# Second attention: the multiplication of the probabilities by their inverse sums moves from VectorE to GpSimd

## The reference, cut to what matters

```python
def _L1_xattn_ref(q, kv, x_seqlens, Wq, Wk, Wv, Wo, q_norm_w, k_norm_w):
    DIM, HEADS, HEAD_DIM = (128, 16, 64)
    qh = (q @ Wq).reshape(b, l, HEADS, HEAD_DIM).transpose(0, 2, 1, 3)
    kh = (kv @ Wk).reshape(b, s, HEADS, HEAD_DIM).transpose(0, 2, 1, 3)
    vh = (kv @ Wv).reshape(b, s, HEADS, HEAD_DIM).transpose(0, 2, 1, 3)
    qh = rms_norm(qh, q_norm_w)          # x * rsqrt(mean(x^2) + 1e-5) * w, over a head's 64
    kh = rms_norm(kh, k_norm_w)
    scores = jnp.einsum('bhld,bhsd->bhls', qh, kh) * (1.0 / np.sqrt(HEAD_DIM))
    scores = jnp.where(mask, scores, NEG_INF)
    attn = jax.nn.softmax(scores, axis=-1)
    o = jnp.einsum('bhls,bhsd->bhld', attn, vh)
    return o.transpose(0, 2, 1, 3).reshape(b, l, HEADS * HEAD_DIM) @ Wo
...
x = x + tanh(g_xattn[1]) * _L1_xattn_ref(_layernorm(x), ctx_1024, _lenS2, ...)
```

## Time and profile before

| what | value |
|---|---|
| median of 3 runs | 2186.36 us |
| the 3 runs | 2183.57 to 2186.93 us |
| the profiled execution: its own time | 2186.99 us |
| the profiled execution: its span | 2185.2 us |
| PE busy, share of the span | 1930.7 us, 88% |
| DVE busy | 1592.2 us, 73% |
| ACT busy | 811.0 us, 37% |
| POOL busy | 662.1 us, 30% |
| second attention, first probabilities turned to last | 842.1 to 1320.1 us |

### The profile page before, as it was taken

How to read it: one execution, slowest core, us unless ns; L and a number is a source line. 1 busy time by engine, 2 the same in 40 slices (tenths; PEclk the granted TensorE clock), 3 DMA queues, 4 the chain that set the end, 5 groups by cost and what they waited for, 6 DMA issues and landing times. The chain is left out here.

```text
span 2185.2 us, 41654 instructions
## 1 busy us (share of the span) xinstructions
PE 1930.7 (88%) x14275; PEld 1025.3 (47%) x14275; DVE 1592.2 (73%) x3255; ACT 811.0 (37%) x1491; POOL 662.1 (30%) x903
## 2 busy tenths in 40 slices
PE   4659998998998978999999998979997999979965
PEld 2644444444444434555555554435663444436631
DVE  4768868878878866777777775757884666658978
ACT  4632112012012105555565553315652222226645
POOL 4551102102102104555555553445730000022301
PEclk8559999999999989999999999989997999999966
DMA  4402222222222231000000000000002533311001
GB/s 112 147 18 60 54 45 59 52 45 59 52 45 59 54 83 65 2 2 1 0 0 0 0 2 1 1 6 16 15 6 63 138 79 105 85 38 19 15 1 39
DMA packets 60079, 89.66 MB, mean 41 GB/s; under 512 B 23720, under 2 KB 42024, under 8 KB 55472
## 3 DMA queue, kind: packets, MB, share of 16 engines
q1 hardware_dynamic: 59952, 88.04, 16.4%
HBM read 80.85 MB, written 2.97 MB: 38 GB/s over the span
## 5 line engine op out<-in xcount | busy, mean ns | idle before, releaser
L1021 PE MATMUL l0f_acc<-l0f_z,w_all 128*128 128x512 f32 x512 | 228.8, 609 | 15.0 <-DVE l0f_z L1229 15.0
L916 POOL TENSOR_TENSOR l0f_v<-l0f_val,l0f_top 64x256 f32<-64x256 f32 x128 | 78.2, 611 | 488.1 <-DVE l0f_val L1191 479.5
L970 PE MATMUL l0f_work<-w_all,l0f_xs 128*128 128x512 f32 x384 | 183.5, 600 | 15.2 <-DVE l0f_val L1186 14.5
L1021 PEld LDWEIGHTS l0f_acc<-l0f_z,w_all 128*128 128x128 f32 x512 | 99.1, 195 | 144.1 <-issue 124.2
L241 POOL TENSOR_SCALAR var_eps<-mean_var 128x4 f32<-128x4 f32 (+1 forms) x64 | 14.6, 227 | 474.3 <-DVE mean_var L225 472.2
L1415 PE MATMUL l1x_proj_v<-l1x_wvo,l1x_cs 128*64 128x512 f32 x512 | 134.9, 605 | 0.1
L1191 DVE COPY_PREDICATED l0f_val<-l0f_oh,l0f_work 128x512 f32<-128x512 int32 x160 | 116.6, 729 | 23.7 <-PE l0f_work L970 7.5
L2826 DVE TENSOR_TENSOR l2f_hu<-l2f_act_g,l2f_pu 128x512 f32<-128x512 f32 x104 | 71.1, 684 | 68.8 <-ACT l2f_act_g L2752 67.4
L2752 ACT ACTIVATE l2f_act_g<-l2f_pg 128x512 f32<-128x512 f32 x104 | 61.5, 594 | 149.8 <-PE l2f_pu L2693 138.0
L2701 PE MATMUL l2f_acc<-l2f_hid,w_all 128*128 128x512 f32 x208 | 107.6, 599 | 10.3 <-DVE l2f_hid L2832 10.3
L1641 DVE TENSOR_TENSOR l1x_nm_q<-l1x_proj_q,l1x_rs_q 128x512 f32<-128x512 f32 x64 | 44.2, 691 | 90.3 <-POOL l1x_rs_q L1351 90.3
(11 more groups left out here) (389 smaller groups left out, 4413.1 us busy)
## 6 DMA issues: line engine op xcount, KB each, us to landing
l0f_first_mask<-onehots SPq DMA_DIRECT2D x32, 512.0 KB, 5.7
w_all<-onehots SPq DMA_DIRECT2D x32, 512.0 KB, 11.8
w_all<-combination SPq DMA_DIRECT2D x40, 256.0 KB, 5.3
w_all<-in_weights SPq DMA_DIRECT2D x1, 4640.0 KB, 16.7
l0x_m_b<-running_max SPq DMA_DIRECT2D x16, 256.0 KB, 4.6
w_all<-combination SPq DMA_DIRECT2D x16, 224.0 KB, 4.5
w_all<-combination SPq DMA_DIRECT2D x16, 192.0 KB, 4.2
w_all<-combination SPq DMA_DIRECT2D x16, 160.0 KB, 4.3
```

The lines of the kernel that those rows point to most:

```text
L916: nc.gpsimd.tensor_tensor(v2[a * SEQ:(a + 1) * SEQ, t % 2, b, :, :], val[r, t % 2, :, :].rearrange("p (c a) k -> p c a k", a=2)[:, :, a, : ...
L970: nc.tensor.matmul(value_banks[e % 3][:, :], xs[:, t * P:(t + 1) * P], ve[:, e, :], start=True, stop=True).then_inc(ve_done, 1)
L1021: nc.tensor.matmul(acc[:, :], oe[:, n % E, n // E, :], z[:, n % Z, :], start=(n == 0), stop=(n == C * E - 1)).then_inc(acc_done, 1)
```

## The change

scale_probs leaves VectorE's program and becomes an instruction of GpSimd. On VectorE the slot loses one instruction, and on GpSimd the slot gains one, ahead of inverse_q, so behind the two inverse roots of the slot before. It waits there for inv_done, and signals prob_ready, as VectorE's did. Operands, shapes and types are the same.

```diff
@@ GpSimd @@
+                def scale_probs(n):
+                    pool.wait_ge(inv_done, count(n + 1))
+                    nc.gpsimd.tensor_tensor(prob[:, :, :], prob[:, :, :], bcast(inv[:, :], 2, SEQ), ALU.mult)\
+                        .then_inc(prob_ready, 1)
+
                 def slot(g, j):
+                    h, i = lagging(g, j, 2)
+                    if live(h):
+                        scale_probs(U * h + i)
                     if live(g):
                         inverse_q(U * g + j)
...
@@ VectorE @@
-                def scale_probs(n):
-                    dve.wait_ge(inv_done, count(n + 1))
-                    nc.vector.tensor_tensor(prob[:, :, :], prob[:, :, :], bcast(inv[:, :], 2, SEQ), ALU.mult)\
-                        .then_inc(prob_ready, 1)
-
...
                     h, i = lagging(g, j, 2)
                     if live(h):
                         totals(U * h + i)
-                        scale_probs(U * h + i)
```

## The result

| | median us | range | runs |
|---|---|---|---|
| before | 2186.24 | 2183.57 to 2189.07 | 10 |
| with the change | 2175.16 | 2167.11 to 2179.32 | 10 |

The account below looks back on a forecast made before the run. TensorE was taken to wait on a circle through VectorE and GpSimd in the second attention. Gains of 12.3 and 0.3 less 1.0 at the ends make 11.6 us: 2186.99 to 2175.4, median-adjusted to 2175; range 2169 to 2187.

Parts of the forecast that it names:

- The bound: Second attention: a circle through VectorE and GpSimd makes TensorE wait 0.59, 1.54, 0.13 us behind copy, residual, xn slots.
- The price: GpSimd's moved multiplication of 128x512 takes 1.04 us, where VectorE took 0.69.
- The rivals of 1.27 and 1.85: GpSimd's multiplication takes 1.27 us: no gain, 2187, chance 0.10; or is held up to 1.85: 2223, chance 0.10.
- The hand-over: From VectorE's reciprocal to GpSimd's multiplication 0.20 us, so start of inv to turn_probs grows from 0.99 to 1.50.
- the copy stretch: From the turn_probs of the copy slot to the next: 7.55 us becomes 7.47, gain 0.08.
- The residual slot: Stretch behind it: addition to x and ms_q move up beside GpSimd's multiplication; 8.50 us becomes 7.89, gain 0.61.
- The norm and the xn slot: Stretches behind them: norm stays at TensorE's 7.23 us, gain 0; xn falls from 7.09 to TensorE's 6.96, gain 0.13.
- The ends: In front of the first and the last turn_probs nothing hides the hand-over: 2 x 0.51 us lost.
- The sum: Second attention: 12.3 us from 15 units, 0.3 from the first unit, less 1.0 at both ends: gain 11.6.
- The other signs: In the profile after, VectorE's idle time before nm_q grows, and proj_q and scores find no new wait.
- The two engines in each other's way: xn slot: GpSimd's multiplication stretches the first xn to 0.75 us, at no cost; rival, pow holds the second: 2186, chance 0.04.
- The twofold price for two inputs: Skill's rule against the move: two-input elementwise work costs GpSimd twice VectorE's time; estimated 1.12 us, sum about 9.

Follow-up runs that it names:

- the run with both moves: Changed kernel with the addition to x behind the sum of squares of q and GpSimd's staging copies behind inverse_k: 2155.11 us, ratio 0.9859 to the kernel before.

## Why the prediction was right, and where its sum was off

*The bound.* Right. The chain through the moved multiplication and GpSimd's inverse root set three of four stretches; with it out of the way TensorE's own 6.96 and 7.18 are what is left (the run with both moves).

*The price.* 1.04, as taken from the broadcast multiplication of line 1814, 64 times within 4 ns. The rivals of 1.27 and 1.85 fall.

*The hand-over.* Mis-sized. 0.20 between VectorE's end and GpSimd's start was taken from ms_q; behind the reciprocal it is 0.08 (900.65 to 900.73, and in all 64 slots). So inv to turn_probs is 1.38, not 1.50, and the copy stretch, which hangs on it in full, is 7.32 instead of 7.47. That is 0.22 of gain instead of 0.08, some 2 us over 15 units.

*The residual slot.* Predicted 7.89, measured 7.73 where the slots are written out, 0.12 of it the hand-over. In the loop it is 7.98. There the addition starts 0.24 to 0.26 after inv, where it is 0.12 in the written-out slots; before, it started 0.61 after the multiplication in both:

```profile
1017.95 0.20 DVE L1678 RECIPROCAL l1x_inv<-l1x_tot 128x8 f32<-128x8 f32 x1
1018.20 0.48 DVE L1683 SCALAR_TENSOR_TENSOR x_all<-l1x_y,tanh_g,x_all 128x256 f32 x1
```

In the loop the tile of x is given by a register (core.x[:, bass.ds(2 * pair, 2), :]), so the likely cause is address work that the multiplication used to cover; register work isn't in the profile, and no run isolates it. The prediction read its rows in written-out slots alone and has no such term. Another 0.1 goes between the addition's start and the end of ms_q (2.03 written out, 2.16 in the loop), most of which was there before too (2.07, 2.15). Against 8.50 to 8.58 the gain is 0.6 to 0.8, near the forecast 0.61, as the two errors are of opposite sign.

*The norm and the xn slot.* 0.13 forecast for xn, 0.13 measured as a mean, though from 7.10 (7.19 in some units) to 7.02, not to 6.96: the stretch begins with a turn that waited. The norm stretch gained 0.06 by its median and 0.1 as a mean where nothing was forecast. The prediction took its 7.23 for TensorE's own time; but that turn was released by the probabilities and took 0.66, and now they are there before TensorE is, it takes 0.60, and 7.18 is left. Also, five of the stretches before were 7.37 or 7.38, which the one unit of the earlier trace rows doesn't show.

*The ends.* Right in kind: the first turn_probs is 0.4 later after the first projection (19.65 to 20.06), and the last stretch is 0.4 longer (6.61 to 7.00). Another 0.35 came behind the last turn_probs.

*The sum.* 11.6 forecast for the stage, 15.6 measured. Summed over the stretches of each kind (the last norm stretch is in the ends, the first unit in the kinds):

| | residual | copy | xn | norm | first unit | ends |
|---|---|---|---|---|---|---|
| forecast | 9.2 | 1.2 | 2.0 | 0 | 0.3 | -1.0 |
| measured | 10.0 | 3.1 | 2.1 | 1.6 | | -1.2 |

By the prediction's own account the hand-over counts in 15 copy slots, 15 residual slots and at two ends: 32 x 0.12 = 3.8, nearly the whole difference. What the norm slots gave and what the loop took in the residual slots about cancel. The hit on 2175 is luck in part: the rest of the program lost some 4 us, which offset the 4 that the stage gained beyond the forecast. The prediction says that nothing outside the stage moves; in that it was wrong. The term of the sum that was mis-sized is the 0.20.

*The other signs.* The idle time before nm_q was to grow on VectorE, as it would have less to do and wait for the same pow. It fell (us in all, times, longest; the first line before, from 850 to 1310, the others after, from 850 to 1300):

```profile
DVE l1x_nm_q L1641 <- POOL l1x_rs_q L1351: 86.8, 61, 1.7
...
DVE l1x_nm_q L1649 <- POOL l1x_rs_q L1351: 67.2, 61, 1.6
DVE l1x_ms_k L1644 <- ACT l1x_sq_k L1554: 18.2, 31, 0.6
DVE l1x_ms_q L1639 <- ACT l1x_sq_q L1549: 15.9, 32, 0.6
```

VectorE is now early enough to wait for ScalarE's squares before both sums, which it never did in this part of the kernel before. No new wait of proj_q or of the scores came up, as was said.

*The two engines in each other's way.* The first xn of a pair took up to 556 ns instead of 345, so it is held:

```profile
L233 DVE TENSOR_SCALAR xn<-x_all,mean_var,rstd x30: 355/366/556, 879.8 to 1291.8; 128x128 f32 x20, 128x128 f32<-128x128 f32 x10
```

All 15 first ones ended 0.08 behind the end of the multiplication, as forecast in kind. That is less than the 0.75 forecast, and ms_k had slack; the stretch behind the xn slot is TensorE's own. By the page SBUF — State Buffer of the Trainium skill (Who interferes with whom), whichever of the two engines issues first has the shared pair for its whole instruction. The trace agrees for the multiplication. For the pow the changed kernel can't tell, as no xn runs beside one there, and the kernel before shows in this stage only xn that began ahead of it. The run in which VectorE multiplies behind ms_q can: its second xn of each pair starts under a pow with 1.6 us to go (the pair, then the pow), and all 15 took 337 to 343 ns, so this pow doesn't hold them:

```profile
911.20 0.60 DVE L233 TENSOR_SCALAR xn<-x_all,mean_var,rstd 128x128 f32<-128x128 f32 x2
...
911.42 1.64 POOL L1351 TENSOR_TENSOR l1x_rs_q<-l1x_ms_q,minus_half 128x8 f32<-128x8 f32 x1
```

The twofold price for two inputs of the page GPSIMD Engine Reference of the Trainium skill (section 3.1) was 1.5-fold here, 1.04 against 0.69.

## What to carry to other kernels

Ask of an instruction not how busy its engine is but what is queued behind it and who waits for that: an addition to x that stood ahead of a sum cost more by its place than the whole multiplication, and moving the sum ahead of it gained 17.7 us where another engine gained 11. Moving work to a slower engine paid here because that engine was idle between the producer and its own next instruction, with nothing else queued ahead; one place later in the same queue, behind an instruction with a wait of its own, the kernel was 232 us slower. Take the hand-over between two engines from the same kind of producer, read rows in the loop as well as in written-out slots, and compare stage with stage, since the rest of a program can move by some us by itself.

## What the runs showed of the hardware

- A start on GpSimd behind VectorE differs by the producer: 0.08 us behind the reciprocal of 128x8 (all 64, changed kernel), 0.20 behind the sum that writes ms_q from 128x512 (all 64, kernel before).
- In the changed kernel 32 turns started 0.05 or 0.06 behind the probabilities; all but the very first took 0.65 or 0.66 us. The 32 that found them ready took 0.60 to 0.63.
- VectorE's float32 xn (tensor_scalar, 128x128) ended 0.08 us behind a multiplication of GpSimd's under which it began (15 of 15, changed kernel), and took its usual 0.34 under a pow (15 of 15, VectorE's multiplication behind ms_q).
- With TensorE busy 469.70 of 650 us the granted clock was 0.92, with 438.18 of 450 it was 1.00.
- Code that nobody touched took 1680.5 to 1688.4 us, with 281 to 302 us at 1.2 GHz in it.
